# Token DMAs in groups of eight, and the last six experts loaded in one go, in a routed-expert attention block

## The reference

```python
def _L0_attn_ref(x, Wq_sem, Wk_sem, Wq_geo, Wk_geo, Wv, Wo, logit_scale):
    ...
    q_geo = _rope(q_geo, pos, ROPE_BASE)
    k_geo = _rope(k_geo, pos, ROPE_BASE)
    remote = Tq - LW
    nblk = remote // MB
    pool = lambda a: jnp.concatenate([a[:, :, :remote].reshape(Bq, HKV, nblk, MB, a.shape[-1]).mean(axis=3), a[:, :, remote:]], axis=2)
    k_sem2, k_geo2, v2 = (pool(k_sem), pool(k_geo), pool(v))
    ...
    probs = jax.nn.softmax(scores, axis=-1)
    out = jnp.einsum('bhqk,bhkd->bhqd', probs, v2)
    ...
def _L0_ffn_ref(x, router_w, expert_bias, gate_proj, up_proj, down_proj):
    ...
    top_w, top_idx = jax.lax.top_k(scores, TOP_K)
    top_w = top_w / jnp.sum(top_w, axis=-1, keepdims=True)
    g = jnp.einsum('bsh,khe->bske', x, gate_proj)
    u = jnp.einsum('bsh,khe->bske', x, up_proj)
    act = jax.nn.silu(g) * u
    out = jnp.einsum('bske,keh->bskh', act, down_proj)
    sel = jnp.take_along_axis(out, top_idx[..., None], axis=2)
    return jnp.sum(sel * top_w[..., None], axis=2)
...
xn = _layernorm(x, axis=-1)
x = x + _L0_attn_ref(xn, ...) + _L0_ffn_ref(xn, ...)
```

## Time and profile before

| | us |
|---|---|
| median of 3 runs | 432.4 (431.57 to 433.18) |
| the profiled execution's own time | 431.69 |
| its span | 429.8 |
| mean granted TensorE clock | 0.953 |
| TensorE matmul busy | 366.6 (85%) |
| VectorE busy | 252.8 (59%) |
| ScalarE busy | 186.3 (43%) |
| GpSimd busy | 242.8 (56%) |

### The profile page before, as it was taken

How to read it: one execution, slowest core, us unless ns; L and a number is a source line. 1 busy time by engine, 2 the same in 40 slices (tenths; PEclk the granted TensorE clock), 3 DMA queues, 4 the chain that set the end, 5 groups by cost and what they waited for, 6 DMA issues and landing times.

```text
span 429.8 us, 8599 instructions
## 1 busy us (share of the span) xinstructions
PE 366.6 (85%) x2259; PEld 307.9 (72%) x2260; DVE 252.8 (59%) x816; ACT 186.3 (43%) x537; POOL 242.8 (56%) x211
## 2 busy tenths in 40 slices
PE   0599996799989998995269999999999999988970
PEld 0574475578857776684258999999999999887860
DVE  4888236799348989995037555555555555444530
ACT  1541246555313552223464555555555555445430
POOL 3502565665653559910199855865655755546573
PEclk9999998989999999799569999999999999999995
DMA  8990212121249540168702866876865766547453
GB/s 249 360 301 24 87 63 88 63 86 64 75 142 327 167 156 26 43 183 233 197 25 45 131 102 110 120 112 100 125 103 98 116 105 109 95 79 121 49 54 45
DMA packets 49015, 51.36 MB, mean 119 GB/s; under 512 B 5472, under 2 KB 46048, under 8 KB 48992
## 3 DMA queue, kind: packets, MB, share of 16 engines
q0 software_dynamic: 14640, 19.34, 27.1%
q1 hardware_dynamic: 34352, 31.74, 26.3%
HBM read 29.63 MB, written 21.43 MB: 119 GB/s over the span
## 4 chain that ended last, share of the span: by engine, by line
PE 62%; DVE 12%; DMA 9%; issue 6%; ACT 4%; SPq 3%; POOLq 2%; POOL 1%; another core or an unknown queue 0%; DVEq 0%; ACTq 0%
PE bank L1235 52%; DMA out_rows<-y,idx 6%; PE bank L1594 3%; PE bank L1612 3%; ACT wgu_hi L714 1%; DMA xg<-xn_by_expert 1%; DMA x_all<-in_L_attn_x 1%; DVE l L1055 1%; ACT x_all L663 1%; PE bank L1359 1%; POOL out_rows L641 1%; DVE idx L1223 1%; DVE lmax L1058 1%; PE bank L1247 1%; DVE q L1028 1%
## 5 line engine op out<-in xcount | busy, mean ns | idle before, releaser
L641 POOL DMA_INDIRECT out_rows<-y,idx x79 | 122.0, 1545 | 71.0 <-DMA out_rows<-y,idx 24.7
L619 POOL DMA_INDIRECT xn_by_expert<-x_all,slot_i x64 | 65.9, 1029 | 20.4 <-issue 15.7
L1235 PE MATMUL bank<-wgu_hi,xh 128*128 x158 | 66.1, 418 | 7.0 <-DVE xl L1214 4.0
L1219 DVE SCALAR_TENSOR_TENSOR act<-bank,xg,sg 128x224 f32<-128x224 f32 x79 | 35.5, 450 | 56.6 <-ACT sg L812 51.3
L1214 DVE TENSOR_TENSOR xl<-bank,xh 128x256 fp32r<-128x256 f32 x79 | 33.5, 424 | 50.7 <-ACT xh L803 41.3
L1235 PE MATMUL bank<-wgu_lo,xh 128*128 x158 | 59.4, 376 | 0.0
L1235 PE MATMUL bank<-wgu_hi,xl 128*128 x158 | 58.9, 373 | 0.0
L1235 PE MATMUL bank<-wdn_hi,ah 112*128 x158 | 51.5, 326 | 1.7 <-DVE al L1227 1.1
L812 ACT ACTIVATE sg<-bank 128x224 f32<-128x224 f32 x79 | 28.3, 358 | 55.3 <-PE bank L1235 49.2
L825 ACT COPY y<-bank 128x256 f32<-128x256 f32 x79 | 29.5, 374 | 43.1 <-PE bank L1235 23.1
L1235 PE MATMUL bank<-wdn_hi,al 112*128 x158 | 44.4, 281 | 0.0
(11 more groups left out here) (218 smaller groups left out, 733.3 us busy)
## 6 DMA issues: line engine op xcount, KB each, us to landing
xg<-xn_by_expert SPq DMA_DIRECT2D x79, 129.0 KB
wgu<-in_L_ffn_gate_proj SPq DMA_DIRECT2D x16, 224.0 KB, 5.5
wgu<-in_L_ffn_up_proj SPq DMA_DIRECT2D x16, 224.0 KB, 5.8
wdn<-in_L_ffn_down_proj SPq DMA_DIRECT2D x16, 224.0 KB, 6.5
x_all<-in_L_attn_x SPq DMA_DIRECT2D x8, 256.0 KB, 5.2
xr<-in_L_attn_x SPq DMA_DIRECT2D x16, 128.0 KB, 8.2
out_rows<-xr SPq DMA_DIRECT2D x16, 128.0 KB
out_rows<-y,idx POOLq DMA_INDIRECT x79
```

The source lines that it names most:

```text
L619: gp.indirect_dma_start(xs_d, bass.IndirectOffsetOnAxis(slot_i[:, z, r:r + 1], 0), x_all[:, z, :], None).then_inc(xs_in[q], DMA)
L641: gp.indirect_dma_start(out_rows, bass.IndirectOffsetOnAxis(idx[r % RING][:, 0:1], 0), ysb[r % 4][:, :], None, compute_op=ALU.add).then_in ...
L1219: nc.vector.scalar_tensor_tensor(av[t.par][:, :], bank[2 + t.par][:, I:2 * I], xg[t.slot][:, D + 1:D + 2], sg[t.par][:, :], ALU.mult, ALU. ...
L1235: return nc.tensor.matmul(o, lhsT, rhs, start=start, stop=stop)
```

## The change

GpSimd sends the tokens in groups of eight DMAs: two groups q share a copy and are waited for together, after both have been issued. SyncE issues pairs 3, 4 and 5 directly one after the other at i = 4, where it issued pair 3 alone, before `store_sum(4)`; pair 4 no longer stands behind `load_residual(6)`, nor pair 5 behind `store_sum(5)`. ScalarE casts experts 10 and 11 in lap 6, and only 12 to 15 at the start of the tile loop.

```diff
-        SPLITS = ((), (4, 5), (6, 7), (8, 9), (), (), (), (10, 11, 12, 13, 14, 15))
+        SPLITS = ((), (4, 5), (6, 7), (8, 9), (), (), (10, 11), (12, 13, 14, 15))
...
                 if i == REMOTE - 3:
                     for q in range(GROUPS):
                         sp.wait_ge(xs_in[q], K * GT * DMA)
-                    load_pair(3)
+                    for n in range(3, (E - EARLY) // 2):
+                        load_pair(n)
                 store_sum(i)
                 if i + 2 < REMOTE:
                     load_residual(i + 2)
-                if i >= REMOTE - 3 and i < REMOTE - 1:
-                    load_pair(i)
...
             for r in range(K):
                 gp.wait_ge(weights_ready, r + 1)
-                for q in range(GROUPS):
-                    nc.gpsimd.tensor_copy(x_all[:, q * GT:(q + 1) * GT, D + 1], weight[:, r, q * GT:(q + 1) * GT]).then_inc(meta_ready, 1)
-                    gp.wait_ge(meta_ready, r * GROUPS + q + 1)
-                    for z in range(q * GT, (q + 1) * GT):
-                        gp.indirect_dma_start(xs_d, bass.IndirectOffsetOnAxis(slot_i[:, z, r:r + 1], 0), x_all[:, z, :], None).then_inc(xs_in[q], DMA)
-                    gp.wait_ge(xs_in[q], (r + 1) * GT * DMA)
+                for h in range(0, GROUPS, 2):
+                    nc.gpsimd.tensor_copy(x_all[:, h * GT:(h + 2) * GT, D + 1], weight[:, r, h * GT:(h + 2) * GT]).then_inc(meta_ready, 1)
+                    gp.wait_ge(meta_ready, r * GROUPS // 2 + h // 2 + 1)
+                    for q in range(h, h + 2):
+                        for z in range(q * GT, (q + 1) * GT):
+                            gp.indirect_dma_start(xs_d, bass.IndirectOffsetOnAxis(slot_i[:, z, r:r + 1], 0), x_all[:, z, :], None).then_inc(xs_in[q], DMA)
+                    for q in range(h, h + 2):
+                        gp.wait_ge(xs_in[q], (r + 1) * GT * DMA)
```

## The result

The changed kernel took 444.5 us (median of 4 runs, 443.47 to 445.84), beside 432.79 us for the kernel before (4 runs, 431.57 to 436.35): ratio 1.0273, 95% interval 1.0233 to 1.0313. The forecast was 428.4 us with a range of 423.9 to 433.0.

A forecast was written before the change was run, and what follows sets the result against it. It took nearly full VectorE and TensorE in the laps, the hand-over to the tiles, then TensorE's matmuls as the bounds; +3.0 - 1.0 - 2.8 - 2.7 - 0.5 + 0 = -4.0 us gave 428.4 us, range 423.9 to 433.0.

The forecast's parts named there:

- rival d: Token DMAs: landing of eight takes what the waits gave, splitting stays put, hand-over still gives 4.0: 428.4 us; chance 0.48 (with forecast).
- the bound of 5.67 us: Token DMAs: upper bound for each of the eight remaining landing waits, from one wait while SyncE's loads filled the queues.
- GpSimd's token part: Token DMAs before the splitting: eight waits and copies go, 15 us earlier, not on the path by itself.
- Splits of 4 to 9: GpSimd's splitting of experts 4 to 9 moves into laps 2 and 3: no change, bounds -4.5 and +4.5 us.
- Rival (b): Laps 2 and 3: splitting causes a second VectorE stall and TensorE's clock falls, +6.4 us, 434.8 us; chance 0.09.
- Lap 6: GpSimd's splitting of experts 10 and 11 delays VectorE's two-operand operations there: +3.0 us, bounds 0 and 4.5.
- just covered: Lap 6's residual, issued at 198.3 and landed about 200.4, in time for VectorE's last additions; at worst 1 to 2 us late.
- the 202: Lap 6: the prediction is wrong if the residual lands behind 202 us.
- Tile load after the last addition: Hand-over: without pair 5 to issue, SyncE issues the first tile load 1.0 us sooner, bounds 0 and 1.1.
- Its landing: Hand-over: first tile load lands in 2.2 us instead of 4.99 with an empty queue, 2.8 us less, bounds 0 and 3.2.
- Two casts fewer: Hand-over: two of ScalarE's six pairs of casts leave it for lap 6, 2.7 us less on the path.
- First tiles: Start of the tiles: one tile fewer hit by GpSimd's splitting, 0.5 us less, bounds -1.5 and +1.5; first scatter about 225.

The follow-up runs named there:

- e10: Kernel before with only GpSimd's part of the change (tokens in groups of eight, waited for together): 432.13 us, ratio 0.9998.
- e14: The same kernel as e10, run again in another batch: 432.10 us, ratio 1.0031 to the kernel before.
- e13: The changed kernel, unaltered, measured again in a later batch: 429.25 us, ratio 0.9939 to the kernel before.
- e16: The changed kernel, unaltered, measured once more after e13 in another batch: 430.06 us, ratio 0.9943 to the kernel before.
- e18: e11 with pair 3 alone loaded at its place and pairs 4 and 5 issued behind lap 6's residual load: 452.38 us, ratio 1.0466.
- e17: The same kernel as e11, measured again in a later batch: 428.07 us, ratio 0.9899 to the kernel before.
- e9: Kernel before with token groups of eight and rows of half the length, so it computes something else: 430.49 us (one run).
- e6: Kernel before with eight token DMAs before the landing wait, and twelve small GpSimd memsets after the fourth: 432.10 us, ratio 0.9984.
- e11: Changed kernel, but GpSimd waits for each group of four token DMAs only after issuing the next four: 427.40 us, ratio 0.9866 to the kernel before.
- e2: Kernel before with only SyncE's pairs 3 to 5 in one go and experts 10 and 11 cast in lap 6: 428.96 us, ratio 0.9925.

## Why the prediction was wrong

**The step that failed.** "I take nothing, since the transfers still follow one another 1.3 us apart. This gain is not on the path by itself." I asked only what eight DMAs in flight do to each other's landing (rival d, and the bound of 5.67 us), and what follows them on GpSimd. I never asked what GpSimd's wait did for the engines beside it, in the stage in which the token DMAs are issued. None of the four rivals places anything before the first lap, and the 17.4 us are there, 15.7 of them holds. The same eights cost nothing in other batches (e10, e14), so the step fails where holds appear and not everywhere; why they appear stays open. The trace of before held a sign of it that I passed over, and that my rows did not show: one hold of VectorE (2.0 us) and one of ScalarE (1.7 us) near 82 us, both "remote" in a program of one core.

**The hand-over came out, the laps did not.** e13 and e16 are the changed kernel without holds: 429.25 and 430.06 us against 428.4, and both inside the range. Term by term, from the table at the top, first after, then e13:

- GpSimd's token part, taken as 15 us earlier and off the path: last token DMA at 139.7 and 143.8 instead of 158.7; the first split in e13 stands where I had put it, near 147:

```profile
148.12 2.07 POOL L604 TENSOR_TENSOR wgu_lo<-wgu,wgu_hi  x1 [3.37 <-issue]
```

  That the gain is off the path held too: e10 and e14, the eights alone, are at 0.9998 and 1.0031.
- Splits of 4 to 9, taken as nothing, bounds 4.5: to the fourth store -0.46 and +1.08 us. The one long hit is still one in e13 (L1167, 3.90 us, against 3.91), only a lap earlier. In e16 it is 6.66 us on the two multiplications, and the stretch is 2.71 us longer:

```profile
147.70 6.66 DVE L1182 TENSOR_TENSOR pr<-pr,srec 128x224 f32<-128x224 f32 x2
```

  Laps 2 to 4 together (the first store at L532 to the fourth) changed by -3.23, +1.08 and, in e16, +2.45 us: two of the three exceed the 2 us that the prediction itself named as a sign of being wrong. Rival (b), +6.4 us, did not come in any.
- Lap 6, taken as +3.0, bounds 0 to 4.5: +4.6 and +3.4. This term was mis-sized by 0.4 to 1.6 us, and +4.6 is just outside its bounds. The hit was mainly on the pair I named, VectorE in e13, 0.69 us before:

```profile
198.64 3.18 DVE L1182 TENSOR_TENSOR pr<-pr,srec 128x224 f32<-128x224 f32 x2
204.83 0.42 DVE L1189 TENSOR_TENSOR xr<-bank,xr 128x256 f32<-128x256 f32 x1 [3.01 <-DMA xr<-in_L_attn_x]
206.00 0.42 DVE L1189 TENSOR_TENSOR xr<-bank,xr 128x256 f32<-128x256 f32 x1 [0.75 <-PE bank L1236]
```

  The second line is the residual that I had put at "just covered": its load was issued at 202.73, not 198.3, since the store before it landed 7.5 us after its issue and not 1.8. It landed near 204.8, behind the 202 that the prediction named as a sign of being wrong; I had the flood's last bytes down by 197 and the store right behind them, and that step was wrong. e18 takes that wait away (its last additions wait 2.48 and 0.96 us for TensorE alone), and the stretch from the fourth store to the last addition becomes 23.75 us, against 24.17 in e13 and 25.12 in e17. So by this comparison across batches the residual is worth 0.4 to 1.4 us of it; the rest stays with the split, 3 us over the 20.78 of before, as forecast. It did not hide under the split, as I had it: VectorE waited 3.01 us for it.
- Tile load after the last addition, -1.0: -1.12 and -1.13. SyncE's queue in e13, with the load on its heels:

```profile
195.25 1.18 SPq L532 DMA_DIRECT2D out_rows<-xr  x2
202.73 0.81 SPq L527 DMA_DIRECT2D xr<-in_L_attn_x  x2
203.59 3.19 SPq L532 DMA_DIRECT2D out_rows<-xr  x4
208.18 3.71 SPq L560 DMA_DIRECT2D xg<-xn_by_expert  x4
```

- Its landing, -2.8: to the first xh -2.97 and -2.84. In e13 TensorE takes up the first tile 2.20 us after its load was issued at 208.18, against 4.99 us for the landing in the earlier trace rows; I had taken 2.2. The chain has the load of the second tile:

```profile
210.38 0.69 PE L1595 MATMUL bank<-const_k,xg 128*128 128x128 f32 x2 [4.41 <-DMA xg<-xn_by_expert]
```

```profile
209.32 2.00 DMA xg<-xn_by_expert
```

  The Trainium skill's figures (page "DMA: Bandwidth & Descriptors", section "Anatomy of one DMA") gave an estimate of 2.3. The section states them for DMAs that GpSimd issues, and this load is SyncE's; the traces lie 0.1 to 0.3 us below it.
- Two casts fewer, -2.7: -1.99 and -2.16. The second xh now waits 0.6 us for TensorE, since the second tile's load was issued 1.1 us behind the first; before, both tiles were there when ScalarE began.
- First tiles, -0.5, bounds -1.5 to +1.5: -1.56 and -1.09, and -2.92 in e16. The first scatter in e13 is at 227.72 and in e16 at 229.64, not 225.

The sum in e13 is -2.7 us on the span and in e16 -2.6; forecast -4.0. In the first measurement the same terms give -3.5 us, and the 17.4 us stand against them. That the sums lie so close together is in part luck: in e16 the laps lose 6.3 us (2.71 and 3.59) and the tiles win 2.9, where I had +3.0 and -0.5.

**The chances.** I gave "slower" 0.09, by one mechanism in the laps. The range holds the changed kernel's time in both later batches in which it ran, and misses it where the holds appear. What was missing was not a size but a rival: that a longer run without a wait can harm the engines beside it.

**What stays open.** What a batch with holds is: the chip alone it is not, since the fifth and sixth ran on the same one, and one of them had holds. What holds the signals: the long holds are all of instructions that wait for another engine, and the longest, in e18, ends as GpSimd pauses (the longest with eights, 4.56 us, does not); whether it is GpSimd's issuing, the transfers, the signals of their landing or the tracing is not shown. e9, with half the bytes, ran in a batch without holds and tells nothing on it. That a gap of any kind helps (e6) is likewise untested where it matters. I found no way to call up the holds at will.

**The fastest kernel** seen is e11 (sliding wait and SyncE's part): 427.4, 427.7 and 428.1 us in three batches, ratios 0.9866 to 0.9909; the intervals of its ratios reach into that of e2. e18 warns against it: it issues the same sixteen in one go, and in a batch with holds took 452. The kernel that can be recommended is e2: GpSimd in groups of four, SyncE's part alone, 428.96 us and 0.9925 in a batch that had holds.

## What to carry to other kernels

Removing a wait can harm engines other than its own; before removing one, ask who works beside it, and count a rival for that. Here it was long runs of GpSimd's DMAs next to a stage that lives on quick hand-overs. Idle time that a single-core profile puts down to "another core" or "remote" is a warning even where it is 2 us long. And a result that a whole batch shows can belong to the batch: run the same kernel again in another one before explaining it.

## What was not expected of the hardware

- The same changed kernel took 443.47 to 445.84 us in one batch and 427.45 to 431.87 and 427.95 to 433.68 us in two others, with the kernel before at 432.35 to 433.58 us beside it.
- Beside 16 token DMAs of GpSimd in one go, ScalarE stood still for 13.05 us, 11.1 of them behind the end of the transposes that it needed, and TensorE started its instructions 1.42 us apart instead of back to back; with eight in one go the longest standstill was 4.58 us, with four 3.1.
- Behind such idle time the granted clock had a mean of 0.66 in the window from 90 to 100 us, part of it thus at the lower of TensorE's two levels (2.4 and 1.2 GHz); without holds (e13) it was 0.83 there. In e18 it was 0.50, the lower level throughout, from 100 to 120 us.
- Two short multiplications of VectorE that met GpSimd's tensor operations took 6.66 us in e16, where they take 0.69 alone.
- A store of 128 KB, issued behind 18 weight DMAs, held back the load that waits for it until 7.5 us after its issue; alone it took 1.80 us.
